# A delta-rule attention kernel: the state update as 16 block-diagonal products instead of 64 small ones

## What is computed

```python
rk = x.reshape(Bb, Tt, H, dd)
rk = rk / jnp.maximum(jnp.linalg.norm(rk, axis=-1, keepdims=True), 1e-12)
wk = jnp.pad(rk[:, :-1], ((0, 0), (1, 0), (0, 0), (0, 0)))
v = (x @ Wv.T).reshape(Bb, Tt, H, dd)
...
def step(S, inp):
    rk_t, wk_t, v_t, g_t, b_t = inp
    pred = jnp.einsum('bhk,bhkd->bhd', wk_t, S)
    err = (v_t - pred) * b_t[..., None]
    S = S + wk_t[..., None] * err[..., None, :]
    o = jnp.einsum('bhk,bhkd->bhd', rk_t, S) * g_t[..., None]
    return (S, o)
...
return out @ Wo.T
```

## Time and profile before

| | us |
|---|---|
| median of 3 runs | 2392.36 |
| lowest and highest | 2385.09, 2395.34 |
| the profiled execution | 2363.46 |
| its span, first to last instruction | 2361.7 |
| granted TensorE clock over the span, mean | 0.968 |

### The profile page before, as it was taken

How to read it: one execution, slowest core, us unless ns; L and a number is a source line. 1 busy time by engine, 2 the same in 40 slices (tenths; PEclk the granted TensorE clock), 3 DMA queues, 4 the chain that set the end, 5 groups by cost and what they waited for, 6 DMA issues and landing times. The chain is left out here.

```text
span 2361.7 us, 145902 instructions
## 1 busy us (share of the span) xinstructions
PE 2096.4 (89%) x61989; PEld 1329.8 (56%) x61989; DVE 1985.9 (84%) x5809; ACT 1726.4 (73%) x3628; POOL 1725.6 (73%) x3096
## 2 busy tenths in 40 slices
PE   1679999999999999999999999999999987399997
PEld 1346666656666666666566666666666655255554
DVE  5388989889888899989888889889888985588886
ACT  2766877778777787787787878778777743477775
POOL 1677888888888888888888888888888853144343
PEclk7789999999999999999999999999999997799999
DMA  2111222222222222222222222222222221478885
GB/s 81 50 49 55 80 74 78 76 76 77 76 76 76 77 76 79 77 77 81 74 78 77 77 73 78 77 75 82 77 76 77 60 60 49 152 198 232 228 230 130
DMA packets 132138, 215.53 MB, mean 91 GB/s; under 512 B 31352, under 2 KB 31360, under 8 KB 131488
## 3 DMA queue, kind: packets, MB, share of 16 engines
q1 hardware_dynamic: 131488, 206.20, 30.2%
HBM read 104.40 MB, written 67.11 MB: 73 GB/s over the span
## 5 line engine op out<-in xcount | busy, mean ns | idle before, releaser
L769 DVE TENSOR_TENSOR ps_elim<-ps_elim,sys 128x30 f32<-128x30 f32 (+14 forms) x1920 | 542.5, 325 | 0.8
L777 DVE TENSOR_TENSOR sys<-sys,ps_elim 128x30 f32<-128x30 f32 (+14 forms) x1920 | 533.9, 315 | 1.0
L894 PE MATMUL ps_v<-wv,xt 128*128 128x512 f16 x1536 | 428.5, 389 | 24.6 <-DMA kbd<-kt 12.6
L894 PE MATMUL ps_y<-wo,ot 128*128 128x512 f16 x1536 | 402.4, 385 | 12.1 <-DVE x L821 9.3
L921 PEld LDWEIGHTS ps_chain<-rhs,t_t 32*32 32x32 f32 x16384 | 263.2, 144 | 127.2 <-issue 125.5
L921 PE MATMUL ps_chain<-rhs,t_t 32*32 32x32 f32 x16384 | 295.0, 218 | 19.9 <-issue 13.9
L678 ACT ACTIVATE state<-ps_s 128x512 f32<-128x512 f32 x128 | 76.4, 597 | 262.2 <-PE ps_s L985 262.1
L915 PEld LDWEIGHTS ps_chain<-state,key_t 32*32 32x32 f32 x16384 | 174.5, 105 | 150.9 <-issue 148.9
L985 PEld LDWEIGHTS ps_s<-err,key_b 32*32 32x32 f32 x16384 | 172.0, 106 | 142.7 <-issue 142.2
L1260 PE MATMUL ps_f<-wq,f_xq 128*128 128x512 f16 x1024 | 242.6, 381 | 6.8 <-DVE f_xq L1232 6.8
L915 PE MATMUL ps_chain<-state,key_t 32*32 32x32 f32 x16384 | 210.8, 195 | 38.2 <-issue 37.7
(11 more groups left out here) (152 smaller groups left out, 5029.1 us busy)
## 6 DMA issues: line engine op xcount, KB each, us to landing
x_in<-in_L_attn_x SPq DMA_DIRECT2D x128, 256.0 KB
kbd<-kt SPq DMA_DIRECT2D x512, 64.0 KB, 2.0
x_res<-in_L_attn_x SPq DMA_DIRECT2D x128, 256.0 KB
x_scratch<-x SPq DMA_DIRECT2D x128, 256.0 KB, 6.4
f_x<-x_scratch SPq DMA_DIRECT2D x32, 1024.0 KB, 7.7
out<-f_res SPq DMA_DIRECT2D x128, 256.0 KB, 3.7
gate<-gates SPq DMA_DIRECT2D x128, 7.9 KB
gate<-gates SPq DMA_DIRECT2D x128, 0.2 KB
```

The lines of the kernel that those rows point to most:

```text
L769: dve.tensor_tensor(tmp, factors(r, c, first, end)[:, c - first:C - 1 - first, c - first:c - first + 1].to_broadcast(shape), sys[:, r, c:c ...
L777: dve.tensor_tensor(dst, dst, tmp, ALU.add).then_inc(elim_done[r], 1)
L894: last = pe.matmul(out, lhs[:, a, kb, :], weights[:, w, kb, :], start=(i == 0), stop=(i == 3 * KB - 1))
```

## The change

The update becomes 16 products, one for each head, with all 128 rows: the stationary side is a tile kbb of 128 rows and 4 x 32 columns, in which batch b's rows hold the weighted key in columns 32 b to 32 b + 31 and zeros elsewhere; the moving side is the error of the head, 128 rows by 32 columns. SyncE spreads key_b into kbb by four transfers for each tile, one step ahead of the update (LAG_KT 1), behind kbd and ahead of x_res. kbb is zeroed once. GpSimd weights the key two steps ahead (LAG_KB 2) and not six, VectorE turns it one step ahead and not seven, so key becomes a ring of 8, and key_t and key_b rings of 2. The 16 products stand in one block behind six of the twelve ps_y matmuls.

```diff
+LAG_KB = 2
+LAG_KT = 1
...
+                n, l, live = on(base, j, LAG_KT)
+                if live:
+                    if n == 0:
+                        sp.wait_ge(s["kbb_zero"], 1)
+                    wait(sp, s["keyb_done"], n + 1)
+                    wait(sp, s["s_psum"], n - 1)
+                    for b in range(B):
+                        sp.dma_start(kbb[C * b:C * b + C, l % 2, :, b, :],
+                                     heads(key_b[C * b:C * b + C, l % 2, :])).then_inc(kbb_loaded[l % 2], 16)
...
-                    wait(pool, s["keyt_done"], n - 1)
-                    wait(pool, s["kt_psum"], n - 1)
-                    wait(pool, s["keyb_done"], n - 1)
-                    pool.tensor_tensor(heads(key[:, l % 2, :]), heads(x_hat[:, l % 4, :]), spread(rn[:, l % 2, :]),
+                    wait(pool, s["keyt_done"], n - 7)
+                    wait(pool, s["kt_psum"], n - 7)
+                    wait(pool, s["keyb_done"], n - 7)
+                    pool.tensor_tensor(heads(key[:, l, :]), heads(x_hat[:, l % 4, :]), spread(rn[:, l % 2, :]),
...
-                    wait(pool, s["s_psum"], n - 7)
...
-                    pool.tensor_tensor(heads(key_b[:, l, :]), heads(key[:, l % 2, :]), spread(beta),
+
+                n, l, live = on(base, j, LAG_KB)
+                if live:
+                    wait(pool, kbb_loaded[l % 2], halves(base, j, LAG_KB) * (16 * B))
+                    pool.tensor_tensor(heads(key_b[:, l % 2, :]), heads(key[:, l, :]), spread(gates[:, l, 0:H]),
...
-                n, l, live = on(base, j, LAG_V)
+                n, l, live = on(base, j, LAG_KT)
                 if live:
                     wait(dve, s["key_done"], n + 1)
-                    wait(dve, s["pred_psum"], n - 7)
-                    wait(dve, s["gram_psum"], n - 7)
-                    dve.transpose(key_t[:, l, :, :], heads(key[:, l % 2, :])).then_inc(s["keyt_done"], 1)
+                    wait(dve, s["pred_psum"], n - 1)
+                    dve.transpose(key_t[:, l % 2, :, :], heads(key[:, l, :])).then_inc(s["keyt_done"], 1)
...
-                    wait(pe, s["keyb_done"], n + 1)
+                    wait(pe, kbb_loaded[l % 2], halves(base, j, 0) * (16 * B) + 16 * B)
...
-                output(0, SHARE - 1)
+                output(0, 2 * SHARE - 1)
                 update_ready(base, j)
-                output(SHARE - 1, SHARE)
-                update(0)
-                output(SHARE, 2 * SHARE)
-                last = update(1)
-                if live:
+                output(2 * SHARE - 1, 2 * SHARE)
+                if live:
+                    for h in range(H):
+                        e = slice(HD * h, HD * h + HD)
+                        last = pe.matmul(ps_s[:, e], kbb[:, l % 2, h, :, :].rearrange("p b e -> p (b e)"), err[:, l % 2, e],
+                                         start=(n == 0 and h == 0), stop=True, skip_group_check=True)
                     last.then_inc(s["s_psum"], 1)
```

More of the change, by code:

```diff
@@ L298, in attention @@
         gate = sb("gate", [P, 8, H])
-        key = sb("key", [P, 2, D])
-        key_t = sb("key_t", [P, 8, H, C])
+        key = sb("key", [P, 8, D])
+        key_t = sb("key_t", [P, 2, H, C])
         kt = sb("kt", [P, 2, KB, P])
         kbd = sb("kbd", [P, 2, HB, KB, P])
-        key_b = sb("key_b", [P, 8, D])
+        key_b = sb("key_b", [P, 2, D])
+        kbb = sb("kbb", [P, 2, H, B, HD])
         b_mask = sb("b_mask", [P, C, H])
@@ L339, in attention @@
         kbd_loaded = [sem(f"kbd_loaded{i}") for i in range(2)]
+        kbb_loaded = [sem(f"kbb_loaded{i}") for i in range(2)]
         gate_done = [sem(f"gate_done{i}") for i in range(8)]
@@ L345, in attention @@
             ss_sum ss_done ln_done rn0_done rn_sq rn_half rn_three rn_done v_psum g_psum v_done gexp_done gden_done gates_done gate_moved
-            key_done keyt_done kt_psum kt_done kbd_zero keyb_done bmask_done gram_psum gram_done mt_done
+            key_done keyt_done kt_psum kt_done kbd_zero kbb_zero keyb_done bmask_done gram_psum gram_done mt_done
             sys_done diag_done tt_done
@@ L454, in _ @@
             pool.memset(kbd[:, :, :, :, :], 0.0).then_inc(s["kbd_zero"], 1)
+            pool.memset(kbb[:, :, :, :, :], 0.0).then_inc(s["kbb_zero"], 1)
             pool.memset(gates[:, BODY - 1, :], 0.0).then_inc(s["first_gate"], 1)
@@ L846, in step @@
                     wait(dve, s["keyb_done"], n - 7)
+                    wait(dve, s["bmask_done"], n - 7)
                     wait(dve, s["o_done"], n - 7)
@@ L914, in predict @@
                         for h, q, e in blocks(half):
-                            last = pe.matmul(ps_chain[q, e], key_t[q, l, h, :], state[q, l % 2, e], start=True, stop=True)
+                            last = pe.matmul(ps_chain[q, e], key_t[q, l % 2, h, :], state[q, l % 2, e], start=True, stop=True)
                         return last
@@ L971, in step @@
                     for kb in range(KB):
-                        last = pe.transpose(ps_v[:, P * kb:P * kb + P], key[:, v_l % 2, P * kb:P * kb + P], k["ident"][:, :])
+                        last = pe.transpose(ps_v[:, P * kb:P * kb + P], key[:, v_l, P * kb:P * kb + P], k["ident"][:, :])
                     last.then_inc(s["kt_psum"], 1)
@@ L980, in output @@
                         return project(ps_y[:, :], ot[:, y_l % 2], k["wo"], range(first, end))
-                def update(half):
-                    if live:
[L984 to L987, removed]
                 if y_live:
```

## The result

| | before | after |
|---|---|---|
| median, us | 2392.34 | 2639.81 |
| lowest and highest | 2385.09, 2395.34 | 2636.27, 2646.22 |
| the profiled execution, its span | 2363.46, 2361.7 | 2646.22, 2644.5 |
| granted TensorE clock, mean of the span | 0.968 | 0.908 |

What follows compares the result with a forecast made beforehand. SyncE's queue was to become the bound in place of TensorE: 112 steps x 1.62 us = +181, TensorE's +0.1 hidden, so 2363.46 + 181 = 2544 us for the profiled execution, 2573 on the median; range 2480 to 2800.

Steps and rivals of the forecast that it cites:

- TensorE's side: The update on TensorE: 1.9 us added, 1.8 removed, net +0.1 us a step, between 0 and +1.7.
- The main term, SyncE's queue: Four kbb issues add 2.86 us to SyncE's 13.4, making 16.26; the step grows 1.62 us over 112 steps, +181 us.
- the rigid part: SyncE's queue from x_res's issue to the second gate issue: some 9.8 us, all pushed by what is put ahead of x_res.
- Two of its signs: SyncE's wait for kt gone in most steps; TensorE waiting for kbd 1 to 1.5 us a step.
- I take 0.06, since the longer stream of the turn fills the rest of the 0.11: Price chosen for each load and matmul pair of the update: 0.06 us, 1.9 us a step; upper end 0.11, 3.5.
- The lower end: Least price of an update pair on TensorE: the load alone, 0.06 us from the turn of key, 1.9 us a step.
- (a): Rival: TensorE's weight loads at 0.11 us a pair, update 3.5 us, on all 128 steps: +218, 2610 us; chance 0.12.
- A credit of 0.23 us a step: TensorE's halts for want of instructions at the update's line, 29.6 us over 43 cases, taken as gone.
- (b): Rival: kbb's small pieces are dear, 4.9 us of issues or x_res starting late: +410, 2802 us; chance 0.15.
- (c): Rival: SyncE has room, kbb costs it under 1.24 us a step: -38 to +13 us, 2354 to 2405; chance 0.13.
- (d): Rival: TensorE's 16 products wait for kbb, which would have to take 9 us to land; no chance of its own.
- The zero for GpSimd: GpSimd's new wait for kbb to land ahead of key_b: a 13.5 us loop under 16.3, so no cost.

Runs made afterwards that it cites:

- e3: The changed kernel without the four kbb transfers and GpSimd's wait for them, kbb staying zero: 2583.87 us, 1.0868 of the kernel before.
- e1: The kernel before plus the four kbb transfers at the changed kernel's place, into a tile nobody reads (unread sums in half precision): 2609.25 us, 1.0955.
- e7: The changed kernel with key_b, kbb and err in half precision: 2575.14 us, 1.0824 of the kernel before.
- e4: e3 with 64 columns of kbb loaded and not 128, from the second tile on: 2305.12 us, 0.9688 of the kernel before.
- e5: e3 with 64 columns of err streamed per product and not 32: 2468.39 us, 1.0357 of the kernel before.
- e6: e3 with the update's products spread in groups between the ps_y matmuls: 2459.82 us, 1.0338 of the kernel before.
- e2: e1 with the kbb transfers issued between the 127-row gate transfer and the wait for it, not behind kbd: 2418.47 us, 1.0161.
- f1: e7 with SyncE's order changed to gates first, then x_in, x_res and x_scratch, then kbd and kbb: 2294.65 us, 0.9632 of the kernel before.
- f3: f1 with x_in moved behind kbb in SyncE's order: 3126.62 us, 1.3116 of the kernel before.
- e8: e7 with the kbb transfers issued between the 127-row gate transfer and the wait for it, not behind kbd: 2352.06 us, 0.9883.
- f2: f1 with x_res and x_scratch moved behind kbb in SyncE's order: 2429.59 us, 1.0183 of the kernel before.

## Why the prediction was right and where it was wrong

**Direction and range.** Slower was right, 2640 us is in 2480 to 2800, and the forecast of 2573 is 67 us low. That it is so near is in part luck: TensorE's side was put at +0.1 us a step and is +1.76 by itself (e3's 16.41 against 14.65). The error hardly shows, because the queue's side, itself put 47 us too low, runs beside it. Without the queue's part the same sum would have said +13 us, where e3 measured +202.

**The main term, SyncE's queue.** It was real but not alone. The issues were right (2.68 us for four, 2.86 forecast), the rigid part too (9.71 us, 9.8 forecast). Where nothing else bounds, e1 and e7, the queue's step is 16.8 us, 16.26 forecast: 0.5 short, since the issues of kbd and kbb are not always the shortest (e1's kbb took 3.71 us in one step, 2.67 in the next). The price alone is 228 us, forecast 181. Two of its signs failed in after: SyncE still waits for kt in 68 steps, and TensorE does not wait 1 to 1.5 us for kbd. The second fails even in e1: the way into TensorE is x_res, VectorE's x1 and the ps_y bank. The prediction pushed x_res behind kbb and never asked who waits for it.

**The step that failed: "I take 0.06, since the longer stream of the turn fills the rest of the 0.11".** A pair costs 0.109 us, the upper end. The lower end came from the turn of key, where the load starts 0.06 us ahead of its matmul, which is not how long it takes; in these products a pair takes 0.11 at 128 loaded columns and 0.06 at 64 (e4), and it takes 0.11 with 32 or 64 columns streamed (e5). The Trainium skill (TensorE: Matmul & The Clock Gate, LDWEIGHTS) gives a load as its columns over 1.2 GHz; an estimate by it is 107 ns for 128 and 53 for 64. The trace agrees at 128 columns (0.109 a pair) and is a little above it at 64 (0.062). The rival (a) built on it was given 0.12, against a row of another operation.

**What neither had: the clock.** Neither the forecast nor (a) costed the granted clock behind the block, 0.88 us a step by e5 and 0.86 by e6, some 111 us in all.

**The halts for instructions.** A credit of 0.23 us a step was taken, at the update's line alone. All lines together went from 116 to 9 us in e3, 0.83 a step. TensorE's side is then 4.79 - 2.91 = +1.88 us a step for the update with its ps_y matmuls, -0.83 for the halts and +0.87 for the clock: +1.92, where the step grew by 1.76. The 0.16 us between them, 20 over 128 steps, stay open.

**Rivals.** (a)'s price for a pair was right, and so was its remark that the two hide each other; its 2610 is the nearest of the forecasts, by a sum without the clock and with too little for the halts, two errors that work against each other. (b) falls: behind kbd, four transfers of 512 pieces are issued in 2.7 us (3.7 at times in e1). (c) falls: e1 has no room. (d) fell too: TensorE has no row of waiting for kbb in after. The zero for GpSimd holds for after, 16.8 us of waiting for kbb; it is 276.5 in e7, where SyncE is the bound.

## What to carry to other kernels

Cost a small matmul by its weight load, from a row of its own shape and precision: 16 fp32 products of 128 columns cost more here than 64 of 32 rows by 32 columns, because a load of 128 columns costs 0.109 us a pair and a small one 0.012 (0.75 us for 64 pairs). By the number of columns alone the small one would be 0.027. When a change loads two resources at once, measure each alone: here either alone costs over four fifths of the whole, so that mending one gives back under a quarter. And for a queue, list for each transfer that is pushed back who waits for it, and look at what stands ahead of the transfer that it waits for; here its order alone moved the time by 191 us down (e1 to e2), 280 down (e7 to f1) and 832 up (f1 to f3).

## What the runs showed of the hardware that was not expected

- The granted clock falls to 0.50 behind a block of 32 fp32 loads of 128 columns with 32-column streams, while TensorE shows no idle time. Its mean from 200 to 1800 us is 0.93 in after and e3, and 1.00 where the loads have 64 columns (e4), where the streams have 64 columns (e5) and where the same products stand in five groups between ps_y matmuls (e6).
- A load of 128 columns in half precision with its matmul takes 0.030 us (e7, 0.48 us for 16) and 0.025 (f1, 0.40 for 16, where the ps_y matmuls ahead run at 2.4 GHz), against 0.109 in fp32, of which each product needs two.
- Four transfers of 512 pieces hold SyncE for 2.7 to 3.7 us behind kbd (after, e1, e7) and for 7.7 to 8.4 us behind x_in and x_res (e2, e8). A transfer of 127 short rows lands 1.85 us after SyncE begins to wait with kbd and kbb ahead of it (f1), 4.8 with x_in ahead (f3), 5.2 with x_res (f2) and 6.9 with both (e7), each the mean of 128.
